# Counting finished node groups on SyncE while a count matrix is built, with four rounds per register load and the clearing transfers moved

## The reference, cut to what matters

```python
w = dinv[row] * dinv[col]
for _ in range(num_steps):              # four times
    x = segment_sum(w[:, None] * x[row], col)
```

## Time and profile before

| what | value |
|---|---|
| median of three runs | 5223.35 us |
| span of the profiled execution | 6351.7 us |
| stage steps, in the profile | 125 to 226 us |
| stage build, in the profile | 226 to 721 us |
| stage hops, in the profile | 721 to 1145 us |

### The profile page before, as it was taken

How to read it: one execution, slowest core, us unless ns; L and a number is a source line. 1 busy time by engine, 2 the same in 40 slices (tenths; PEclk the granted TensorE clock), 3 DMA queues, 4 the chain that set the end, 5 groups by cost and what they waited for, 6 DMA issues and landing times. The chain is left out here.

```text
span 6351.7 us, 75027 instructions
## 1 busy us (share of the span) xinstructions
PE 2842.1 (45%) x17919; PEld 2271.2 (36%) x17920; DVE 3726.5 (59%) x6870; ACT 1728.7 (27%) x5084; POOL 3463.1 (55%) x3375
## 2 busy tenths in 40 slices
PE   4544588433343334477614434434431343444442
PEld 1333456223333333345403333333331233333332
DVE  6444544255555666444426776667673767667678
ACT  0255200011111111000003354344340335445434
POOL 5667445466555663544265565566525556556551
PEclk7655699666666666678855555555555555555555
DMA  3720400355555554400021111111102111111110
GB/s 101 171 94 1 127 1 1 105 154 172 167 171 169 173 173 143 139 4 1 8 49 42 37 42 37 37 41 38 33 10 50 40 37 42 37 39 41 41 30 13
DMA packets 470914, 446.71 MB, mean 70 GB/s; under 512 B 113322, under 2 KB 417773, under 8 KB 470268
## 3 DMA queue, kind: packets, MB, share of 16 engines
q1 hardware_dynamic: 230602, 227.94, 12.4%
q0 software_dynamic: 116768, 136.51, 9.0%
q10 hardware_dynamic: 123282, 79.08, 4.5%
HBM read 306.93 MB, written 136.34 MB: 70 GB/s over the span
## 5 line engine op out<-in xcount | busy, mean ns | idle before, releaser
L2412 POOL DMA_INDIRECT tg<-tab_d,tail_ids x1632 | 1711.2, 1049 | 1191.1 <-DVEq L2731 644.9
L458 POOL DMA_INDIRECT sorted_edges_d<-place_batch x784 | 825.0, 1052 | 657.1 <-issue 220.6
L2437 PE MATMUL hr<-near_table,near_hot 128*128 x4896 | 654.4, 278 | 926.2 <-issue 593.1
L1598 POOL DMA_INDIRECT xg<-tab_d,src_i x784 | 768.0, 980 | 501.1 <-issue 241.6
L2445 PE MATMUL acc<-msg,sum_hot 128*96 128x65 f32 x3264 | 559.8, 364 | 902.1 <-ACT msg L2519 701.3
L2437 PEld LDWEIGHTS hr<-near_table,near_hot 128*128 128x128 f16 x4896 | 505.6, 108 | 1075.7 <-issue 970.2
L2445 PEld LDWEIGHTS acc<-msg,sum_hot 128*96 128x96 f32 x3264 | 536.4, 277 | 924.8 <-issue 924.7
L2492 ACT ACTIVATE pr<-hr 128x396 f32<-128x396 f32 x576 | 272.2, 482 | 1235.0 <-DMA b2col<-in_L_gnn_be_dram 786.9
L2513 ACT ACTIVATE pr<-pr,coef_c 128x64 f32<-128x64 f32 x1496 | 380.7, 340 | 82.4 <-issue 79.4
L2506 ACT ACTIVATE msg<-tg,coef_b 128x64 f32<-128x64 f32 x1632 | 399.1, 340 | 2.6 <-DVEq L2926 2.6
L2743 DVE TENSOR_REDUCE scal<-prod 128x17 f32<-128x1088 f32 x288 | 370.5, 1286 | 9.8
(11 more groups left out here) (504 smaller groups left out, 5392.9 us busy)
## 6 DMA issues: line engine op xcount, KB each, us to landing
ex<-spread_d SPq DMA_DIRECT2D x112, 448.0 KB
msg_d<-back ACTq DMA_DIRECT2D x112, 448.0 KB
near_hot<-head_row_d SPq DMA_DIRECT2D x96, 408.0 KB
tg<-tab_d,tail_ids POOLq DMA_INDIRECT x1632
spread_d<-zeros ACTq DMA_DIRECT2D x28, 896.0 KB
spread_d<-zeros SPq DMA_DIRECT2D x28, 896.0 KB
idsU<-dst_short_d SPq DMA_DIRECT2D x112, 224.0 KB
pairs_d<-pair_m SPq DMA_DIRECT2D x3, 4800.0 KB
```

Source lines behind the costliest of these rows:

```text
L458: l.eng.indirect_dma_start(K.sorted_edges[:, :], bass.IndirectOffsetOnAxis(ap=K.batch[:, n % 2, 0, k:k + 1], axis=0), K.batch[:, n % 2, 1, ...
L1598: l.eng.indirect_dma_start(xg[j.c % ROWS][:, half * H + k, :], None, K.tab1, bass.IndirectOffsetOnAxis(ap=src_i[:, t:t + 1], axis=0)).then ...
L2412: e.indirect_dma_start(tg[:, u % TAILS * GQ + k, :], None, K.tab3, bass.IndirectOffsetOnAxis(ap=K.tail_ids[:, u * GQ + k:u * GQ + k + 1], ...
L2437: ins = e.matmul(hr[(u * FILLS + g) % 2][:, c:c + PW3], near_hot[u % HOTS][:, k, :], rows[:, bass.ds(at[k] + n * PW3, PW3)], start=n == 0, ...
```

## The change

SyncE now loads the step counts of the groups and waits for them. After each it adds one to a new semaphore, `grouped`. ScalarE's program becomes straight code of 391 groups that waits on `grouped` against constants and loads no registers. TensorE's loop has 37 turns of four rounds and loads 32 registers in each; `least` is the last of the eight loaded values of a round, and the bank of the eighth step is worked out from it. The ten batches of the build come into a tile of their own by one transfer at the head of the stage, so SyncE no longer fills the tile of two there. The steps stage clears 20 of the 56 pieces of the table in place of 28, the build clears none in place of 28, and ScalarE clears the other 36 in hops. The scatters stay in their stages.

```diff
+TURN = 4
+CLEARED = 20
+HELD = (2, 10)
...
+def loads_until(n):
+    return sum(1 for m in range(n % 2, n + 1, 2) if not HELD[0] <= m < HELD[0] + HELD[1])
...
-def place_batches(l, K, first, count, pace=None, stored=BATCH):
+def place_batches(l, K, first, count, pace=None, stored=BATCH, held=None):
...
-        l.eng.wait_ge(K.queued[n % 2], 16 * (n // 2 + 1))
+        if held is None:
+            l.eng.wait_ge(K.queued[n % 2], 16 * loads_until(n))
+        else:
+            l.eng.wait_ge(held[1], 16)
...
 step_tables
         def scalar(l):
-            for n in range(STEPS // 2):
+            for n in range(CLEARED):
                 clear_rows(l, K, K.spread1, n)
...
-            v.tensor_scalar(K.step_regs[:, :, SG:SG + 1], at_i[...][:, :, SG - 1:SG], 1.0, None, ALU.add)
+            v.tensor_scalar(K.step_regs[:, :, SG - 1:SG], at_i[...][:, :, SG - 1:SG], 1.0, None, ALU.add)
...
-            v.tensor_scalar(K.step_regs[:, :, 0:SG], ring_i[...], 9, None, ALU.logical_shift_left)
+            v.tensor_scalar(K.step_regs[:, :, 0:SG - 1], ring_i[...][:, :, 0:SG - 1], 9, None, ALU.logical_shift_left)
...
 build_pairs
         def gpsimd(l):
-            place_batches(l, K, 2, 10, turned, 4)
+            place_batches(l, K, *HELD, turned, 4, (held, held_in))
         def sync(l):
-            for n in range(10):
-                queue_batches(l, K, 2 + n, 1)
-                for step in range(STEPS // 2 + n * 4, min(STEPS // 2 + n * 4 + 4, STEPS)):
-                    clear_rows(l, K, K.spread1, step)
+            e = l.eng
+            first, lots = HELD
+            e.dma_start(held[:, :, :, :], K.queue[first:first + lots, :, :, :].rearrange("n p two k -> p n two k")).then_inc(held_in, 16)
+            with l.loop(GROUPS // SG) as i:
+                over = load_counts(nc, mybir.EngineType.SP, K.group_ends[0:1, bass.ds(i * SG, SG)], NS + AHEAD)
+                for b in range(SG):
+                    e.wait_ge(stepped, over[b])
+                    e.sem_inc(grouped, 1)
...
         def tensor(l):
-            with l.loop(ROUNDS // 2) as i:
-                both = load_values(nc, mybir.EngineType.PE, K.step_regs[0:1, bass.ds(i * 2, 2), 0:SG + 1],
-                                   0, (SG - 1) * 512)
-                for s in range(2):
-                    *regs, least = both[s * (SG + 1):(s + 1) * (SG + 1)]
+            with l.loop(ROUNDS // TURN) as i:
+                values = load_values(nc, mybir.EngineType.PE, K.step_regs[0:1, bass.ds(i * TURN, TURN), 0:SG],
+                                     0, (SG - 1) * 512)
+                for r in range(TURN):
+                    s = r % 2
+                    *regs, least = values[r * SG:(r + 1) * SG]
                     least = nc.s_assert_within(least, 1, GROUPS)
                     e.wait_ge(emptied, least)
...
-                    e.wait_ge(made, i * 4 + (s + 1) * 2)
+                    e.wait_ge(made, i * (2 * TURN) + (r + 1) * 2)
...
+                    regs.append((least - 1 & SG - 1) << 9)
...
         def scalar(l):
-            turn = 3 * SG
-            with l.loop(GROUPS // turn) as i:
-                for c in range(0, turn, SG):
-                    over = load_counts(nc, mybir.EngineType.Activation, K.group_ends[0:1, bass.ds(i * turn + c, SG)], NS + AHEAD)
-                    for b in range(SG):
-                        a.wait_ge(stepped, over[b])
-                        empty(b, bass.ds(i * (turn * GD) + (c + b) * GD, GD))
...
+            for g in range(GROUPS):
+                a.wait_ge(grouped, g + 1)
                 empty(g % SG, slice(g * GD, g * GD + GD))
...
 hops
+            def scalar(l):
+                for step in range(CLEARED, STEPS):
+                    clear_rows(l, self.K, self.K.spread1, step)
```

More of the change, by code:

```diff
@@ L457, in place_batches @@
                 l.eng.sem_inc(l.sink, 1)
-            l.eng.indirect_dma_start(K.sorted_edges[:, :], bass.IndirectOffsetOnAxis(ap=K.batch[:, n % 2, 0, k:k + 1], axis=0),
-                                     K.batch[:, n % 2, 1, k:k + 1], None).then_inc(K.sent[n % 2], 16)
+            lot = K.batch[:, n % 2, :, :] if held is None else held[0][:, n - first, :, :]
+            l.eng.indirect_dma_start(K.sorted_edges[:, :], bass.IndirectOffsetOnAxis(ap=lot[:, 0, k:k + 1], axis=0),
+                                     lot[:, 1, k:k + 1], None).then_inc(K.sent[n % 2], 16)
             done += 1
@@ L690, in vector @@
             v.tensor_scalar(ring_i[:, :], at_i[:, :], SG - 1, None, ALU.bitwise_and).then_inc(l.sem, l.add(1))
-            v.tensor_scalar(K.step_regs[:, :, SG:SG + 1], at_i[:, :].rearrange("o (r k) -> o r k", k=SG)[:, :, SG - 1:SG], 1.0, None, ALU.add).then_inc(l.sem, l.add(1))
+            v.tensor_scalar(K.step_regs[:, :, SG - 1:SG], at_i[:, :].rearrange("o (r k) -> o r k", k=SG)[:, :, SG - 1:SG], 1.0, None, ALU.add).then_inc(l.sem, l.add(1))
             v.wait_ge(l.sem, l.done())
-            v.tensor_scalar(K.step_regs[:, :, 0:SG], ring_i[:, :].rearrange("o (r k) -> o r k", k=SG), 9, None, ALU.logical_shift_left).then_inc(l.sem, l.add(1))
+            v.tensor_scalar(K.step_regs[:, :, 0:SG - 1], ring_i[:, :].rearrange("o (r k) -> o r k", k=SG)[:, :, 0:SG - 1], 9, None, ALU.logical_shift_left).then_inc(l.sem, l.add(1))
             for n, (at_, w) in enumerate(pieces):
@@ L773, in build_pairs @@
         ring = st.enter_context(nc.psum_tensor(fresh("ring"), [P, SG, 512], F32))
-        counted, clean, made, stepped, emptied, turned = (sem(n) for n in ("counted", "clean", "made", "stepped", "emptied", "turned2"))
+        held = sb("held_batches", [P, HELD[1], 2, BATCH], I32)
+        counted, clean, made, stepped, emptied, turned, grouped, held_in = (
+            sem(n) for n in ("counted", "clean", "made", "stepped", "emptied", "turned2", "grouped", "held_in"))
         def gpsimd(l):
             l.eng.iota(row[:, :], pattern=[[1, KW]], base=0, channel_multiplier=0, allow_small_or_imprecise_dtypes=True).then_inc(counted, 1)
-            place_batches(l, K, 2, 10, turned, 4)
+            place_batches(l, K, *HELD, turned, 4, (held, held_in))
         def sync(l):
-            for n in range(10):
-                queue_batches(l, K, 2 + n, 1)
-                for step in range(STEPS // 2 + n * 4, min(STEPS // 2 + n * 4 + 4, STEPS)):
-                    clear_rows(l, K, K.spread1, step)
+            e = l.eng
[6 more added lines that the diff above has]
+                    e.sem_inc(grouped, 1)
+            over = load_counts(nc, mybir.EngineType.SP, K.group_ends[0:1, GROUPS // SG * SG:GROUPS], NS + AHEAD)
+            for g in range(GROUPS // SG * SG, GROUPS - 1):
+                e.wait_ge(stepped, over[g % SG])
+                e.sem_inc(grouped, 1)
+            e.wait_ge(stepped, NS + AHEAD)
+            e.sem_inc(grouped, 1)
         def vector(l):
@@ L1123, in gpsimd @@
                 place_batches(l, self.K, 12, 7, full[0], 4)
-            drive(nc, "hops", dict(tensor=tensor, vector=vector, sync=sync, gpsimd=gpsimd))
+            def scalar(l):
+                for step in range(CLEARED, STEPS):
+                    clear_rows(l, self.K, self.K.spread1, step)
+            drive(nc, "hops", dict(scalar=scalar, tensor=tensor, vector=vector, sync=sync, gpsimd=gpsimd))
 def wide(col, width=D):
```

7 lines of the change are left out of this document (removed).

## The result

The kernel after takes 5196.33 us, the median of four runs (5191.11 to 5207.73), the kernel before 5222.72. The ratio is 0.9945, 95% interval 0.9933 to 0.9957: 26 us faster, inside the range, but a third of the 73 us that were forecast.

The account below looks back on a forecast made before the run. A loop of waits around TensorE's register loads bounds the build, GpSimd close below. Build 73 plus steps 13 gives 86 us of the profile, 71 if shrunk evenly; 73 was taken: 5223 - 73 = 5150 us, range 5095 to 5203.

Parts of the forecast that it names:

- A gain of 73: Build stage: forecast to take about 422 us where the profile showed 495, a gain of 73 us.
- 42 "irregular" us: Build before: time beyond undisturbed turns and bursts, taken as mostly TensorE waiting for ScalarE; 22 of 42 us kept.
- TensorE's side, 419: Build: TensorE's start, 37 turns of four rounds, added instructions, irregular waits and end, forecast at 419 us together.
- named signs of being wrong: Gaps over 4.6 us, TensorE waiting for ScalarE at most turns, steps still slow, or hops over 10 us longer.
- GpSimd's side, 420: Build: 280 unpaced scatters at 403 us, plus a longer first load, denser compares and barrier, together 420 us.
- Rival (a): Build: register loads cheap in size, GpSimd less slow without the profiler; gain 100 to 130 us, 5105 us; chance 0.20.
- Bursts, 22 us: Build: six TensorE gaps after SyncE's clearing bursts, some 3.6 us extra each, 22 us that the change would remove.
- Hops, 0: Hops: 36 clearing transfers added at no cost; if the cover failed, some 20 us would come back.
- (b): Build: register loads cost fully per register, or SyncE late once in eight groups; near 5190 us; chance 0.16.
- (c): Build: loads cost more than the trace's proportional end, gap 4.6 us or more; 5195 to 5262 us; chance 0.08.
- (d): Build: ring closes over SyncE's loads, 12.0 us per eight groups instead of 9.9; 5313 us, slower; chance 0.06.
- Steps, 13 us: Steps: fewer clearing transfers end TensorE's slow stretch; GpSimd becomes last and the stage ends 13 us earlier.

Follow-up runs that it names:

- e1: The kernel before, unchanged, profiled again at the slow speed: 6298.73 us, build 492.4 us.
- f1: The kernel before, unchanged, profiled again at the quick speed: 5224.27 us, build 455.0 us.
- f4: The kernel before with only the clearing transfers moved, both loops as they were, quick speed: 5191.43 us, ratio 0.9935.
- e3: The kernel before with only the clearing transfers moved, both loops as they were, slow speed: 6304.34 us, ratio 1.0016.
- i3: The changed kernel, unaltered, run at the slow speed: 6308.83 us, ratio 1.0014 to the kernel before.
- h1: The changed kernel with one of the build's ten batches of scatters sent in hops instead, quick speed: 5157.69 us, ratio 0.9862.
- h3: h1 with ScalarE's old loop, which loads its counts itself, and nothing counted on SyncE, quick speed: 5162.66 us, ratio 0.987.
- i1: The changed kernel with one batch of scatters later and two rounds per register load instead of four, slow speed: 6362.42 us, ratio 1.0108.
- f2: The changed kernel, unaltered, run again at the quick speed: 5187.95 us, ratio 0.9931 to the kernel before.

## Why the prediction was right or wrong

The direction and the range held. The size failed at the first step of the sum.

**The build before (the failed step).** "A gain of 73" was 495 less 422. The 422 was nearly right: after takes 426.1. The 495 was taken at the slow speed, and the runs were made at the quick one, where it is 455.0. Nearly all of the 42 "irregular" us, 37 by e1 less f1, belong to the slow speed. The prediction took them mostly for TensorE waiting for ScalarE. By f1 that was wrong: ScalarE's loads are the same there, and the 42 are gone. The prediction had the sign of it in hand (the runs 1.216 times shorter "and no row says where") and weighed only whether the gain shrinks evenly or not at all, 71 or 86. The third case, that what the gain is made of exists only in the slower execution, was left out. The split of the gain was wrong as well. By forecast 22 of the 73 us came from the bursts and 51 from the loops. Measured, the moved clears alone give 28 of the 29 us (f4), so the right direction did not come from the loops.

**TensorE's side, 419.** The period was 10.3 by forecast and 10.45 by measurement, with rounds 1.87 to 1.93 us apart for 1.68 to 1.92 and a gap of 3.24 for 3.5. One of the named signs of being wrong did appear: 25 of the 37 long gaps are put down to ScalarE (L863, the old 837). But they are as long as the 11 that are put down to "issue", 3.24 us, so ScalarE is the name there and not the cause. But the side ended at 388 + 2 = 390 us (611.0 less 222.5), since 22 us were kept for irregular waits and next to none came, and 6.3 us before the first matmul became 4.2. So "the two sides are even" was wrong: TensorE had 36 us to spare, and an easier TensorE could not shorten the stage.

**GpSimd's side, 420.** Its scatters and gaps are 420 us without the barrier. The barrier was 1.4 us in the sum and 5.7 in the trace (642.9 to 648.6); before, TensorE was last, and this end never showed. This is the side that decided. Rival (a) failed on it, as its "against" said.

**Bursts, 22 us.** Right in place and size, by f1 and f4: 455.0 to 427.1, of which 22 are the six gaps and the rest starts and small gaps. It is the only part of the build's gain that the change delivers.

**Hops, 0.** Right at the quick speed (385.8 to 386.0 and 387.1; pacing does nothing). At the slow speed the named failure came, some 20 us, by the one profile e1: 23 in e3, 25 in i3. Against the 423 us of the first profile it is 2 to 4.

**Rivals (b), (c), (d).** (b)'s 5190 is near the measured time, by another mechanism: SyncE was not late by anything that decided, as h1 beats h3. (c) fell with the gap of 3.24. By 18 registers in 2.49 us and 32 in 3.24, a further register adds (3.24 - 2.49) / 14 = 0.05 us to the gap; from the 16 in 2.18 of i1 it is 0.07. What hides under matmuls is not in these figures. The Trainium skill, in Runtime: NRT & Kernel Launch, section Instruction fetch mechanics, gives some 200 ns for each register of a TENSOR_LOAD, even in bulk; the page means loads from HBM (the chip's DRAM), and these come from a tile in SBUF (the on-chip memory). The measurement decides, and for this kind of load it is a quarter to a third of that. (d) fell too: there was no cycle of 12 us.

**Steps, 13 us.** Measured 4 to 8 at the quick speed, 1 at the slow one, and the mechanism was wrong. The forecast took TensorE's slow stretch for late instructions behind full transfer engines. VectorE's last operation, which ends TensorE's and VectorE's side, in f1 (quick, engines full) and in i3 (slow, engines idle), and i3's own TensorE lines in two stretches (us, PE, PEld, PEclk, DMA share, GB/s):

```profile
204.22 0.18 DVE L702 TENSOR_TENSOR degree<-stepps,bases_next 128x25 f32<-128x25 f32 x1 [0.99 <-PE stepps L749]
```

```profile
223.48 0.18 DVE L714 TENSOR_TENSOR degree<-stepps,bases_next 128x25 f32<-128x25 f32 x1 [0.99 <-PE stepps L761]
...
172.00:194.00 22.00, 19.07 (x86) 8.56 (x87) 0.84 1.05 211
194.00:217.00 23.00, 3.64 (x14) 0.92 (x11) 0.64 0.03 1
```

With the engines full TensorE's side ends at 204 in the quick execution. With them at 0.03 its straight code still crawls in the slow one. The slow stretch goes with the slow speed, not with the clearing. The Trainium skill, in Runtime: NRT & Kernel Launch, section Instruction fetch mechanics, calls the cost of crossing from one block of instructions to the next mostly hidden. If these are late instructions, which no row proves, i3's 14 matmuls in 23 us are an exception to it. At the quick speed the stage ended with GpSimd already before. What the change gained there is the end behind the last scatter, in f1, then in after:

```profile
226.56 0.14 DVE L789 MEMSET none<- 128x100 uint32 x1 [22.15 <-PEq L125]
```

```profile
208.95 0.19 DVE L714 TENSOR_TENSOR degree<-stepps,bases_next 128x25 f32<-128x25 f32 x1 [0.99 <-PE stepps L761]
...
210.67 0.96 POOL L470 DMA_INDIRECT sorted_edges_d<-place_batch  x1 [0.30 <-issue]
222.54 0.29 POOL L791 IOTA cell_row<- 128x200 f32 x1 [10.91 <-POOLq L128]
```

GpSimd's sequencer held the stage 14.7 us behind its last scatter with the transfers' engines full (f1), and 5.8 to 10.9 with them idle (h1, f2, f4, after). What it waits for is not named by any row. In f1 the engines' share is still 1.00 from 222 to 224 us, just ahead of the stage's end. That fits scatters that land behind the clearing, but is not shown. "The barrier's 1.4 us" was the end behind VectorE, which is not this one.

## What to carry to other kernels

Before a profiled execution's durations are summed, compare its span with the runs. If they differ by a fifth, the irregular part of a stage is the first suspect, and the period of its undisturbed turns is safer to build on. Here the period of 5.72 us was the same at both speeds and the "issue" gaps were not. Where two engines are found even at the end of a stage, a change to one of them is worth nothing until the other is unloaded as well; one batch moved turned a gain of 37 us (f2) into one of 69 (h1).

## What the runs showed of the hardware

- This program runs in 5225 or in some 6300 us (6286 to 6344), by batch, and one chip number stands beside both. At an equal count of matmuls, TensorE's issue gaps are what grows in the build (58 to 126 us with the change).
- A stage that ends with GpSimd's indirect transfers ended 5.7 to 10.9 us after the last of them even with next to nothing else moving (the build and steps of after), and 14.7 us with the transfer engines full (steps of f1).
- At the head of TensorE's loop, a load of 16 registers came with a gap of 2.18 us, one of 18 with 2.49, one of 32 with 3.24.
- Four transfers of 0.917 MB issued at once stopped TensorE's loop for 3.3 to 4.0 us beyond its usual gap, six times, although no instruction of it waits for them.
